# Message-passing kernel: node rows as two rounded 32-bit pieces, twelve of sixteen edge groups summed with byte matrices

## The reference, cut to what matters

```python
x = _layernorm(x + _L0_gnn_ref(...))   # relu([x[src], edge_attr] @ W1a + b1a) @ W1b, mean over dst, an MLP
x = _layernorm(x + _L1_gnn_ref(...))   # segment_sum(h[src], dst) @ W, a batch norm over all nodes
x = _layernorm(x + _L2_gnn_ref(...))   # mean over dst of x[src], @ W, elu
x = _layernorm(x + _L3_gnn_ref(...))   # twice: sum over dst of weight * x[src] @ W[edge_type]
```

## Time and profile before

| | us |
|---|---|
| median of 3 runs (3955.51 to 3958.72) | 3958.48 |
| the profiled execution, whole device time | 3955.51 |
| its span, from the first to the last instruction | 3955.5 |
| PE busy | 3633.9 (92%) |
| DVE busy | 2106.4 (53%) |
| ACT busy | 1709.5 (43%) |
| POOL busy | 2819.9 (71%) |
| mean granted TensorE clock | 0.959 |

### The profile page before, as it was taken

How to read it: one execution, slowest core, us unless ns; L and a number is a source line. 1 busy time by engine, 2 the same in 40 slices (tenths; PEclk the granted TensorE clock), 3 DMA queues, 4 the chain that set the end, 5 groups by cost and what they waited for, 6 DMA issues and landing times. The chain is left out here.

```text
span 3955.5 us, 73204 instructions
## 1 busy us (share of the span) xinstructions
PE 3633.9 (92%) x25526; PEld 2998.0 (76%) x25526; DVE 2106.4 (53%) x7623; ACT 1709.5 (43%) x4516; POOL 2819.9 (71%) x2949
## 2 busy tenths in 40 slices
PE   7999999999999999699997989899997899989898
PEld 5888888888876777476665777677775888878887
DVE  6988888888873222633335455454542233333332
ACT  4454454545452000411216455555554545444443
POOL 5777777777726777477766777777776777777776
PEclk9999999999999999899998999999997899999998
DMA  7676666767757777577753454455543455455453
GB/s 243 213 217 211 213 212 212 216 208 215 218 158 208 213 212 216 142 221 224 220 169 133 164 170 169 157 173 169 169 165 129 144 160 167 157 166 167 156 167 118
DMA packets 441830, 728.10 MB, mean 184 GB/s; under 512 B 69922, under 2 KB 294050, under 8 KB 441315
## 3 DMA queue, kind: packets, MB, share of 16 engines
q1 hardware_dynamic: 306706, 447.48, 34.5%
q0 software_dynamic: 107536, 248.96, 22.7%
q10 hardware_dynamic: 27202, 26.78, 2.1%
HBM read 530.29 MB, written 192.69 MB: 183 GB/s over the span
## 5 line engine op out<-in xcount | busy, mean ns | idle before, releaser
L635 POOL DMA_INDIRECT work<-table_rel,reli x1462 | 1383.6, 946 | 495.8 <-issue 440.6
L635 POOL DMA_INDIRECT work<-table_pre,srci x831 | 805.7, 970 | 263.8 <-issue 261.7
L2451 ACT ACTIVATE work<-iota,local 128x72 f32<-128x72 f32 x1464 | 378.0, 342 | 339.6 <-PE bank L1500 335.7
L2456 ACT ACTIVATE work<-work,ew,src_lo 128x72 f32<-128x72 f32 x1464 | 514.8, 434 | 6.1
L1500 PE MATMUL bank<-work 128*128 128x72 f32 x2928 | 391.4, 292 | 130.2 <-DMA work<-table_rel,reli 130.0
L1500 PEld LDWEIGHTS bank<-work 128*128 128x128 f32 x2928 | 382.9, 208 | 167.1 <-DMA work<-table_rel,reli 160.0
L1269 PE MATMUL bank<-work,acc 128*128 128x360 f16 x2574 | 439.9, 317 | 26.8 <-DVE acc L1616 18.0
L904 PE MATMUL bank<-w_both,work 128*128 128x256 f32 x1664 | 436.6, 388 | 13.5 <-issue 8.2
L635 POOL DMA_INDIRECT work<-table_mean,srci x311 | 302.7, 973 | 158.5 <-issue 89.0
L916 PEld LDWEIGHTS bank<-work 128*128 128x128 f32 x3328 | 394.9, 192 | 6.2 <-ACT work L1010 1.9
L916 PE MATMUL bank<-work 128*128 128x64 f32 x3328 | 397.3, 273 | 0.3
(11 more groups left out here) (345 smaller groups left out, 5916.5 us busy)
## 6 DMA issues: line engine op xcount, KB each, us to landing
work<-adj SPq DMA_DIRECT2D x104, 720.0 KB
adj<-X SPq DMA_DIRECT2D x130, 450.0 KB
work<-ea_cols SPq DMA_DIRECT2D x208, 256.0 KB
kept<-work SPq DMA_DIRECT2D x50, 880.0 KB
kept<-w_both SPq DMA_DIRECT2D x50, 880.0 KB
work<-kept SPq DMA_DIRECT2D x50, 880.0 KB
w_both<-kept SPq DMA_DIRECT2D x50, 880.0 KB
work<-adj SPq DMA_DIRECT2D x52, 810.0 KB
```

What stands on the lines that cost most here:

```text
L635: pool.indirect_dma_start(into[:, u, :], None, tables[p], bass.IndirectOffsetOnAxis(ap=idx_of(p)[:, t:t + 1].bitcast(U32), axis=0)).then_i ...
L2451: ins = act.activation(hot3[:, u, :], iota[:, 0:PAIR_WIN], ACT.Abs, bias=local[:, t:t + 1], scale=-1.0)
L2456: ins = act.activation(hot3[:, u, :], hot3[:, u, :], ACT.Relu, bias=ew[:, t:t + 1], scale=src_lo[:, t:t + 1])
```

## The change

1. D goes from 10 to 12 and S from 6 to 4: positions 0 to 5 of every eight groups are dense. Pass 0 builds 156 matrices in place of 130. The counts are stored as bytes (`adj` and `stage` in U8).
2. The rows are divided into two pieces of the rounded 32-bit type F32R: ACT rounds (`split_high`), DVE subtracts and rounds (`split_low`). Two steps go. The pieces lie in planes 1 and 2 of `acc`; what pass 1 kept in plane 1 goes to plane 0, the 25 `clear` operations of pass 1 go, and POOL clears plane 0 once before pass 2.
3. SP loads five pieces of a step (ten tiles each, 360 bytes in a row) into a ring of four byte buffers. Ten times per step a part of five tiles (2160 numbers in each partition) is turned into F32R: even parts by ACT, odd ones by DVE, each into one buffer of its own (`counts[n % 2]`). PE multiplies a part by ten products of 432 columns (12 x 36).
4. ACT's work in the passes is now written out step by step (`wide_act`), the conversions placed among the node work, and the places of the node work on PE and DVE move to fit four gathered groups. The dense sums of DVE are taken in two halves of six.
5. Six DVE operations join the check of the edge order at the start. Many buffers move.

```diff
-DENSE = [q for q in range(BODY) if q % SLOTS in (0, 1, 3, 4, 5)]
+NEAR = 6
+DENSE = [q for q in range(BODY) if q % SLOTS < NEAR]
-A_PARTS = ((0, 9, 0), (9, 17, 1), (17, 25, 2), (25, 34, 0), (34, 42, 1), (42, 50, 2))
-A_RING = (9, 8, 8)
-SPLITS = 3
+PARTS, LOADS, A_SLOTS = CHUNKS, CHUNKS // 2, 4
+PARTS_AT = ((0, 1, 2), (3, 4), (5, 6, 7), (8, 9))
...
-        adj = nc.dram_tensor("adj", [WIDE * D, P, NT * AW], FP16).ap()
+        adj = nc.dram_tensor("adj", [WIDE * D, P, NT * AW], U8).ap()
+        piece_hi, piece_lo = (nc.alloc_sbuf_tensor_at(name, [P, NT, F], F32R, offset=acc_at + plane * ACC * 4)
+                      for name, plane in (("piece_hi", 1), ("piece_lo", 2)))
...
+            apart = local[:, :].rearrange("p (g q u) -> p g q u", q=SLOTS, u=U)[:, :, 0:NEAR, :]
+            rises = codef[:, 0:GROUPS // SLOTS * NEAR * (U - 1)]
+            for u in range(1, U):
+                done(dve, dve.tensor_tensor(rises.rearrange("p (g q u) -> p g q u", q=NEAR, u=U - 1)[:, :, :, u - 1],
+                                            apart[:, :, :, u], apart[:, :, :, u - 1], ALU.subtract))
+            done(dve, dve.tensor_reduce(stat[:, DEV:DEV + 1], rises, AX_X, ALU.min))
...
+            if p == 2:
+                pool.wait_ge(m_u, CHUNKS)
+                pool.sem_inc(gate, 1)
+                pool.memset(acc[:, 0, :], 0.0).then_inc(acc_zero, 1)
...
+        def counts_wait(eng, n):
+            eng.wait_ge(raw_ready[n // 2 % A_SLOTS], (n // 2 // A_SLOTS + 1) * 16)
+            if n >= 2:
+                eng.wait_ge(a_used, n - 1)
+        def counts_on_act(act, n):
+            if n % 2 == 0 and n < 2 * WIDE * PARTS:
+                counts_wait(act, n)
+                act.activation(counts_of(n), part_of(n), ACT.Copy).then_inc(act_counts, 1)
+        def counts_on_dve(dve, n):
+            if n % 2 and n < 2 * WIDE * PARTS:
+                counts_wait(dve, n)
+                dve.tensor_copy(counts_of(n), part_of(n)).then_inc(dve_counts, 1)
...
+                pe.wait_ge(dve_counts if n % 2 else act_counts, n // 2 + 1)
+                for t in range(CT):
+                    for x in (piece_hi, piece_lo):
+                        mm = pe.matmul(bank[D_BANKS[step % 2]][:, 0:D * AW], x[:, i * CT + t, :], counts[n % 2][:, t, :],
+                                       start=(i == 0 and t == 0 and x is piece_hi), stop=(i == PARTS - 1 and t == CT - 1 and x is piece_lo))
                 mm.then_inc(a_used, 1)
...
+        def split_high(act, k, of):
+            act.activation(piece_hi[:, k * CT:(k + 1) * CT, :], of, ACT.Copy).then_inc(x_high, 1)
+        def split_low(dve, k, of):
+            own = slice(k * CT, (k + 1) * CT)
+            dve.tensor_tensor(piece_lo[:, own, :], of, piece_hi[:, own, :].bitcast(F32), ALU.subtract).then_inc(x_low, 1)
...
+                if n >= A_SLOTS:
+                    sp.wait_ge(act_counts, n - A_SLOTS + 1)
+                    sp.sem_inc(gate, 1)
+                    sp.wait_ge(dve_counts, n - A_SLOTS + 1)
+                    sp.sem_inc(gate, 1)
+                a_load(sp, n)
```

More of the change, by code:

```diff
@@ L270, in by_pair @@
             return x.rearrange("p (d s) -> p d s", s=PU)
[L272 to L292, removed]
+        raw = [x[:, 0:D * 2 * CT * AW // 4].bitcast(U8).rearrange("p (d c) -> p d c", d=D)
+               for x in (src_both, work[:, 7400:8480], late_lo[:, :, :, :].rearrange("p a c f -> p (a c f)").bitcast(F32),
+                         work[:, 6320:7400])]
         b_rows = view(3840, BT, F)
@@ L1209, in wide_dve, with dense_sums @@
             following = load_bases(dve, 0) + load_bases(dve, BASES)
-            def dense_sums(step, at):
-                dve.wait_ge(a_used, (step + 1) * len(A_PARTS))
-                for i in range(D):
+            def dense_sums(step, at, lo=0, hi=D):
+                if lo == 0:
+                    dve.wait_ge(a_used, (step + 1) * PARTS)
+                for i in range(lo, hi):
                     add_dense(step, at, i)
-                dve.wait_ge(wide_added, step * BODY + early(step) + D)
+                if hi == D:
+                    dve.wait_ge(wide_added, step * BODY + early(step) + D)
+            for i in range(PARTS):
+                counts_on_dve(dve, start * PARTS + i + 2)
             dense_sums(start, following)
@@ L1221, in wide_dve @@
                 for j in range(S):
+                    ready = list(PARTS_AT[j]) if it + 1 < WIDE else []
+                    if j == 0 and it and not early(step):
+                        if ready:
+                            counts_on_dve(dve, (step + 1) * PARTS + ready.pop(0) + 2)
+                        dense_sums(step, at, D // 2, D)
                     for place in ahead(p, it, j):
                         node(dve, it, place)
+                    for i in ready:
+                        counts_on_dve(dve, (step + 1) * PARTS + i + 2)
                     add(step, at, j)
@@ L1233, in wide_dve, with part_of, counts_of, wide_act @@
                 if it + 1 < WIDE and not early(step + 1):
-                    dense_sums(step + 1, following)
+                    dense_sums(step + 1, following, 0, D // 2)
             for j in range(S + 1):
                 node(dve, WIDE, j)
-        LOAD_AT = (0, 3)
+        def part_of(n):
+            at = n % 2 * CT * AW
+            return raw[n // 2 % A_SLOTS][:, :, at:at + CT * AW].rearrange("p d (t c) -> p t d c", c=AW)
+        def counts_of(n):
+            return counts[n % 2][:, :, :].rearrange("p t (d c) -> p t d c", c=AW)
+        def counts_wait(eng, n):
[10 more added lines that the diff above has]
+                dve.tensor_copy(counts_of(n), part_of(n)).then_inc(dve_counts, 1)
+        def wide_act(act, p, node, between):
+            start = (p - 1) * WIDE
+            for i in range(PARTS):
+                counts_on_act(act, start * PARTS + i + 2)
+                if i == 3:
+                    between(act, 0, 0)
+            for it in range(WIDE):
+                step = start + it
+                for j in range(S):
+                    for place in ahead(p, it, j):
+                        node(act, it, place)
+                    for n, i in enumerate(PARTS_AT[j] if it + 1 < WIDE else ()):
+                        counts_on_act(act, (step + 1) * PARTS + i + 2)
+                        if n == 0 and it:
+                            between(act, it, j)
+                for place in behind(p, it):
+                    node(act, it, place)
+        LOAD_AT = (0, 2)
         def wide_pe(pe, p, before, node):
@@ L1280, in wide_pe @@
                         node(pe, it, place)
-                    if it + 1 < WIDE:
-                        dense(step + 1, j)
+                    for i in PARTS_AT[j] if it + 1 < WIDE else ():
+                        dense(step + 1, i)
                     segment(step, j)
@@ L1292, in added_by @@
                 if p == 1 and it == WIDE - 1:
-                    return it * BODY + early(it) + D + sum(q < LIMIT[k] - it * BODY for q in SPARSE) - early(it)
+                    return it * BODY + D + max(early(it), sum(q < LIMIT[k] - it * BODY for q in SPARSE))
                 if p == 1 and LIMIT[k] <= (it + 1) * BODY:
@@ L2390, in node2_pe @@
                 node2_mm(pe, it - 1)
+            if it < WIDE and j == SECOND_AT(it):
+                for k in seconds(it - 2):
+                    rel_pe(pe, 0, k)
             if it == WIDE - 1 and j == 2:
```

382 lines of the change are left out of this document (186 added, 196 removed).

## The result

The changed kernel takes 3967.48 us (median of 20 runs, 3962.57 to 3979.47), the kernel before 3959.27 in its 20 runs beside it. The ratio is 1.0021 with a 95% interval of 1.0015 to 1.0028: slower by 0.2%, where 3860 and a gain of 2.5% was forecast. The profiled execution has a span of 3963.5 us, 8.0 more than before.

What follows compares the result with a forecast made beforehand. POOL was taken to bound pass 0, PE and POOL pass 1, PE pass 2. Terms of -72 (pass 1), -33 (pass 2), +5 (pass 0) and +1 (start) sum to -99: 3860 us, range 3830 to 3925.

Steps and rivals of the forecast that it cites:

- What bounds the kernel before: POOL bounds pass 0, PE and POOL are both full in pass 1, PE bounds pass 2.
- The dense product: Passes 1 and 2 on PE: one pass, 0.183 us for 432 columns, 100 products a step.
- rival 4: Dense product takes more than one pass: two cycles a column give 4284 us, four 5282; chance 0.11.
- ACT's conversion: Passes 1 and 2: ACT turns a part of 2160 numbers a partition in 2.00 us, five a step.
- DVE's conversion: Passes 1 and 2: DVE turns a part of 2160 numbers in 1.27 us; other end 2.42.
- rival 1: DVE converts one element a cycle, 2.42 us; steps of 27.5 and 31.9, +55 us, 3915; chance 0.15.
- Steps: Pass 1 steps 24.7 us, -72 for the pass; pass 2 ten of 30.8 and two of 24.0, -33.
- The wait behind the layer norm: Pass 2: PE waits 4.0 us a step for conversions behind the norm, taken between 0 and 6.1.
- Loads: Passes 1 and 2: 360-byte packets at 24.4 ns by a line between two packet sizes, 11.7 us a step, hidden.
- Rival 3: Loads are late in pass 1: 360-byte packets cost 48.8 ns, +26 us, 3886; chance 0.06.
- Pass 0: 26 more fills: POOL stays the bound by 2%, PE at 98%; +5 us, between 0 and +26.
- rival 2: PE becomes the bound of pass 0: +26 us in place of +5, 3880; chance 0.08.

Runs made afterwards that it cites:

- the early copy: ACT's copy of the third bank put ahead of the relu in pass 0: ratio 1.0004 on the kernel before; on the changed kernel 3932.73 us, ratio 0.9934.
- the order changed: Changed kernel with DVE's conversion written with the 12 groups outermost and the 5 tiles inside: 3894.53 us, ratio 0.9843 to the kernel before.

## Why the prediction was wrong

- **What bounds the kernel before** held: with fewer gathers and fewer columns the steps of passes 1 and 2 fell, and in pass 0, which POOL bounded, the early copy gave the kernel before nothing. But of the 55 us in which PE was not busy there, 51 were waits for ACT's copies. They cost nothing while POOL set the pace; I read them as room.
- **The dense product.** One pass was right (rival 4, at 0.11, did not happen). The term was 0.183 and measured 0.196 us: the overhead of 3 ns was taken from the 16-bit product, and here it is some 16. 100 x 0.013 = 1.3 us a step, 31 us in 24 steps. (A full 32-bit product stands twice in the view: a gathered group's four are "x8" in the earlier trace rows. So the 0.65 us that I read as two products of 256 columns are one, which no term of the sum uses; the rounded product stands there once.) The Trainium skill (FP8 and Floating Point Precision, TensorE Precision Notes) sets reduced 32-bit precision apart from the four passes of the true one; the trace agrees, with 0.196 us for 432 columns against 0.885 for 512 of the full type.
- **ACT's conversion** 2.00 us: measured 2.008.
- **DVE's conversion** is the step that failed: 1.27 us was taken since "these rows are conversions too". They are, but the part has five tiles outermost, and 2.402 us was measured. I had the other end, 2.42, as rival 1 with 0.15. The Trainium skill's rule of outermost dimensions (VectorE: DVE Perf Modes, What auto-detection actually checks) would have made the choice a question before any run, though it decides for 2.42 only when read on merged dimensions. With 1.285 us in its place pass 1 costs -53 and pass 2 -39, together 92 against the 100 forecast.
- **Steps.** With the order changed a step of pass 1 is 25.9 us, nearly the forecast 24.7 and the 1.3 of the slower product. Rival 1 gave 27.5; with 1.3 more that is 28.8, and 28.9 was measured. (Its 2.8 was said to be half of 3.9 + 2.2, which is 3.05.) In pass 2 it gave 31.9 for ten of the steps, and the last ten take 31.9, although the product is slower. The wait behind the layer norm was set too high: with the order changed the last ten take 29.9 us, and 29.9 less 19.6 + 3.5 + 0.9 + 4.0 leaves 1.9 us of waiting, not 4.0. Nor did the 4.0 follow from its own terms, 6.1 less 2.5 being 3.6.
- **Loads.** 93120 packets in 346 us at 39.9% of 16 queues are 23.7 ns each; the line had given 24.4. Rival 3 did not happen. The Trainium skill's limit of 512 bytes (DMA: Bandwidth & Descriptors, Specifications) shows here in no doubling: the packets of 360 bytes cost 0.066 ns a byte, those of 592 bytes 0.058.
- **Pass 0** was the second step that failed: between 0 and +26 I took +5, and +34.5 was measured, beyond the upper end. PE's added products were priced about right: with the early copy PE is busy for 1026 us where 1031 was forecast, and the pass is 5.6 us longer. What the sum lacked is the order on ACT, a copy that stands behind relus that wait for DVE, which the early copy showed to cost 32 us. Rival 2 had the sign but the wrong mechanism, PE's content. (Of codes the sum counted three a fill on DVE; there are four, 1.47 us together, 38 us and not 36.) Which of the added work tips the loop stays open.
- **The chances.** Rival 1 came true, pass 0 grew by more than rival 2 said, and the product was slower: 3860 + 55 + 30 + 31 is 3976, near the 3967 that was measured. The joint case was "left out" of the range though neither rival excludes the other. By the prediction's own numbers it is 3860 + 55 + 20 = 3935, already past the 3925; each alone would have stayed within.

## What to carry to other kernels

Before pricing a conversion on DVE, look at the outermost dimensions of both operands, as written and as they are after merging, and not only at the type: here the same copy takes 2.40 or 1.29 us by the order in which its dimensions are written. Before counting an engine's idle time as room, ask what it waits for in it: waits that cost nothing now become the pace once the present bound moves, and an edit that only changes an order can give them back. Rivals that can happen together need the range of their sum.

## What the hardware showed that was not expected

DVE at two elements a cycle makes POOL's gathers longer. Groups of the kernel with the order changed, 1264 to 1574 us, and of the changed kernel, 1268 to 1614 us:

```profile
L636 POOL DMA_INDIRECT work<-table_gcn,srci x192 | 219.7, 1144 | 90.8 <-issue 53.4 <-PE bank L1314 37.4
```

```profile
L636 POOL DMA_INDIRECT work<-table_gcn,srci x191 | 181.5, 950 | 165.8 <-PE bank L1313 109.7 <-issue 56.1
```

1.144 us in place of 0.950 on the mean. It is the conversions: the 62 gathers that overlap one of DVE's take 1.547 us on the mean (up to 2.02), the other 130 take 0.950. In the changed kernel the 98 that overlap a conversion, there at one element a cycle, take 0.943. Here this is hidden because POOL has time to spare; in a pass that POOL bounds I would expect it to cost, which no run shows.

A wait of PE can also cost clock. Granted clock of the changed kernel ahead of the wait of 1.39 us in the timeline above, behind it, and after that (windows, columns as in the earlier trace rows):

```profile
1356.00:1357.50 1.50, 1.32 (x9) 0.91 (x7) 1.47 (x3) 1.50 (x1) 0.24 (x1) 1.00 0.00 0
1358.90:1362.20 3.30, 3.24 (x9) 3.01 (x10) 0.81 (x4) 0.00 (x0) 2.44 (x3) 0.51 0.78 189
1362.30:1365.00 2.70, 2.70 (x18) 2.61 (x17) 2.25 (x1) 0.31 (x1) 0.00 (x0) 1.00 0.29 78
```

It falls to the lower level, 1.2 GHz, and nine products take 3.3 us where they take 1.8 at the upper one: the wait costs 1.5 us more than its own length. Not every wait does: over the twelve steps of pass 1, with 25 waits for DVE, the clock is 0.99. Over the steps of pass 2 it is 0.97 in the changed kernel and 1.00 both in the kernel before and in the one with the order of dimensions changed.
